# First layer of a five-layer graph network: dense input read from a transposed copy, and a ring of high and low parts scattered by 256-column products

## The chip, the cores and the metric

One core of one Trainium2 chip runs the whole program. The metric is the time of one execution on the device, in microseconds (us). The kernel before took 5494.6 us, the median of three runs (5491.9 to 5495.12).

The engines named here are PE (TensorE, the matrix engine, with PEld for its weight loads), DVE (VectorE), ACT (ScalarE), POOL (GpSimd) and SP (SyncE, which only issues transfers).

## The reference

Five graph layers (SAGE convolutions) run over 100,000 nodes and 50,000 edges that are sorted by destination:

```
def sage(x, Wl, b, Wr):
    mean = segment_sum(x[src], dst) / max(degree, 1)
    return mean @ Wl + b + x @ Wr
x = layernorm(x + sage(relu(sage(x, a1)), a2))
x = layernorm(x + sage(relu(sage(relu(sage(x, b1)), b2)), b3))
```

All values are float32. Layers a1 and a2 are 128 wide, b1 is 128 to 256, b2 is 256 to 256, b3 is 256 to 128. The change is in a1 alone, which has neither a ReLU on its input nor a residual.

## The kernel before

Nodes are cut into 196 groups of 512 (4 tiles of 128). Each layer is one pass over the groups, and the passes run one after the other with a barrier between them. Layers with 128 output columns (a1, a2, b3) are made by `narrow_pass`, those with 256 (b1, b2) by `wide_pass`.

A pass has a dense part and an edge part. Edge tiles of 128 edges are handled two per step. For edge step p, POOL gathers 2 x 128 source rows from HBM by index into `e_rows` (L627), PE transposes them (`turn_edges`, L652), ACT copies the result to `e_full` (L730), PE multiplies by Wl (`project`, L700), and ACT scales by 1/degree and writes the result into a ring of 32 slots in SBUF (`to_ring`, L743). For node group g, SP loads the rows (L580), PE transposes them (`turn_nodes`, L661), ACT copies them (`nodes_full`, L738), and `multiply` (in two halves, u = 0 and 1) adds up in PSUM: 4 dense products with Wr (L686) and 8 scatter products (L690), each a one-hot matrix of 128 x 128 times one slot of the ring. DVE makes the one-hot matrices (`compare`, L792, two of 512 columns for a group) and adds the bias on the way out (`add_up`, L807). SP stores the group (L590).

Edges run 6 steps ahead of nodes (LEAD = 6), so step g works on p = g + 6. What each engine does in a step is written out by hand, and each engine works its own list in order:

- PE: `places(g)` (reads ring slots into registers), `turn_nodes(g+1)`, `multiply(g, 0)`, `project(p-1)`, `turn_edges(p+1)`, `multiply(g, 1)`.
- ACT: `edges_full(p)`, `take_numbers(p+2)` (L725, writes the indices for a gather), `nodes_full(g+1)`, `to_ring(p-1)`.
- POOL: wait for `take_numbers(p+2)`, a marker operation (L623), two gathers for p+2 (L627).
- DVE: `compare(g+1, 0)`, `add_up(g-1)`, `compare(g+1, 1)`.
- SP: load of group g+3, store of group g-1.

`e_rows` has two buffers. `take_numbers(p+2)` comes behind `edges_full(p)` on ACT, and that is what says that a buffer is free. So the gather for p+2 begins in step g and PE takes its rows in step g+1.

Of the kernel before, what the change touches and what calls it, by code (L numbers as in the profile page):

```python
# [12 lines left out]
P = 128  # L13
# [5 lines left out]
LEAD = 6  # L19
BEHIND, AHEAD = 12, 5  # L20
# [494 lines left out]

def narrow_pass(pr, cv):
# [4 lines left out]
    norm = res is not None  # L521
    FUNC = ACT.Relu if cv["relu"] else ACT.Copy
    late = 2 if norm else 1
    with ExitStack() as c:  # L524
        rows_in = pr.sb(c, "m_rows_in", [P, 2, T, kt * P])
        t_full = pr.sb(c, "m_t_full", [P, 2, kt, GROUP])
        onehot = pr.sb(c, "m_onehot", [P, 2, 2 * T, P])
        rows_out = pr.sb(c, "m_rows_out", [P, 2, T, fo])
        e_idx = pr.sb(c, "m_e_idx", [P, 2, 2], I32)
        e_rows = pr.sb(c, "m_e_rows", [P, 2, 2, kt * P])  # L530
        e_full = pr.sb(c, "m_e_full", [P, 2, kt, 2 * P])
        ring = pr.sb(c, "m_ring", [P, RING * fo])
        held = pr.sb(c, "m_held", [1, 1])
        if norm:
# [9 lines left out]
        turned = [pr.ps(c, f"m_turned{i}") for i in range(2)]  # L544
        product = [pr.ps(c, f"m_product{i}") for i in range(2)]
# [3 lines left out]
        rows_here = [pr.counter(f"m_rows_here{i}", 16) for i in range(2)]  # L549
        res_here = [pr.counter(f"m_res_here{i}", 16) for i in range(2)]  # L550
        stored = [pr.counter(f"m_stored{i}", 16) for i in range(2)]
        gathered = [pr.counter(f"m_gathered{i}", 32) for i in range(2)]
        names = ("turned", "full", "onehot", "product", "sum", "stats", "meanvar", "std", "rstd", "shift", "normed",
                 "index", "held", "eturned", "efull", "eproduct", "ring", "eps")
        (s_turned, s_full, s_onehot, s_product, s_sum, s_stats, s_meanvar, s_std, s_rstd, s_shift, s_normed,
         s_index, s_held, s_eturned, s_efull, s_eproduct, s_ring, s_eps) = [pr.counter("m_" + x) for x in names]
        s_done = s_normed if norm else s_sum
        block = c.enter_context(nc.Block())

        def is_last(g):  # L560
            return isinstance(g, int) and g == G - 1

        def has(g, back):

            return g is not None and not (isinstance(g, int) and g < back)

        def turned_before(g, p):

            if p is None:
                return G - 1 if g == G - LEAD else None  # L570
            return None if isinstance(p, int) and p == 0 else p - 1

        def view(t, g, width):
            return t[bass.ds(node_base(pr, g), GROUP), 0:width].rearrange("(t p) f -> p t f", p=P)

        @block.sync
        def _(sp):
            def load_rows(g, s):
                wait(sp, s_turned, (g - 1) * kt)
                sp.dma_start(rows_in[:, s, :, :], view(h, g, kt * P)).then_inc(rows_here[s].sem, 16)  # L580

            def load_res(g, s):
                wait(sp, s_sum, g - 1)
                sp.dma_start(res_in[:, s, :, :], view(res, g, P)).then_inc(res_here[s].sem, 16)

            def store(g, s):
                wait(sp, s_done, g + 1)
                if is_last(g):
                    wait(sp, stored[1 - s], G // 2)
                sp.dma_start(view(out, g, fo), rows_out[:, s, :, :]).then_inc(stored[s].sem, 16)  # L590

            for g in (0, 1):
                load_rows(g, g)
                if norm:
                    load_res(g, g)
            load_rows(2, 0)

            def step(g, s, more):
                if not (isinstance(g, int) and g >= G - 3):
                    load_rows(g + 3, 1 - s)  # L600
                if has(g, late):
                    store(g - late, (s - late) % 2)
                if more and norm:
                    load_res(g + 2, s)

            for g in (0, 1):
                step(g, g, True)
            with sp.Fori(1, G // 2 - 2) as i:
                for s in range(2):
                    step(i * 2 + s, s, True)  # L610
            for g in range(G - 4, G):
                step(g, g % 2, g < G - 2)
            for g in range(G - late, G):
                store(g, g % 2)
# [4 lines left out]
        def _(pool):  # L619
# [5 lines left out]
            def gather(s):  # L625
# [5 lines left out]
            def step(g, p, s, i, j):  # L631
                if p is not None and not (isinstance(p, int) and p + 2 >= G):
                    wait(pool, s_index, p + 3)
                    wait(pool, s_held, p + 1)
                    mark().then_inc(s_held.sem, 1)
                    gather(s)

            mark().then_inc(s_held.sem, 1)
            for p in range(2):
                wait(pool, s_index, p + 1)  # L640
                gather(p)
            steps(pr, pool, step)

        @block.tensor
        def _(pe):
            def turn_edges(p, s, j):
                wait(pe, gathered[s], j + 1)
                wait(pe, s_efull, p)
# [6 lines left out]
            def turn_nodes(g, s, i):  # L655
                wait(pe, rows_here[s], i + 1)
                for k in range(kt):
                    wait(pe, s_full, g * kt + k - 1)
# [6 lines left out]
            def places(g):  # L665

                _, at = nc.values_load_multi_w_load_instructions(
                    pr.t_slot[0:1, bass.ds(g * (2 * T), 2 * T)], engines=[mybir.EngineType.PE], min_val=0,
# [3 lines left out]
            def multiply(g, s, at, u):  # L672
                wait(pe, s_onehot, g * 2 + u + 1)
                bank = product[s]
                if u == 0:
                    ready = g + LEAD - 2
                    wait(pe, s_full, (g + 1) * kt)
                    wait(pe, s_ring, min(ready, G) if isinstance(g, int) else ready)
                    wait(pe, s_sum, g - 1)
                    if norm:  # L680
                        pe.matmul(bank[:, :], pr.two_rows[:, :], cv["bias_row"][:, :, :].rearrange("p a n -> p (a n)"),  # L681
                                  start=True, stop=False, skip_group_check=True)
                for t in range(2 * u, 2 * u + 2):
                    to = bank[:, t * P:(t + 1) * P]
                    for k in range(kt):
                        pe.matmul(to, t_full[:, s, k, t * P:(t + 1) * P], cv["r32"][:, k, :],  # L686
                                  start=(not norm and t == 0 and k == 0), stop=False, skip_group_check=True)
                    for w in range(2):
                        n = 2 * t + w
                        mm = pe.matmul(to, onehot[:, s, n, :], ring[:, bass.ds(at[n] * fo, fo)], start=False,  # L690
                                       stop=(w == 1), skip_group_check=True)
# [3 lines left out]
            def project(p, s):  # L695
                wait(pe, s_efull, p + 1)
                wait(pe, s_ring, p)
# [6 lines left out]
            def step(g, p, s, i, j):  # L704
                if g is None and p == LEAD - 1:
                    turn_nodes(0, 0, 0)
                if g is not None:
                    at = places(g)
                    if not is_last(g):
                        turn_nodes(g + 1, 1 - s, i + s)  # L710
                    multiply(g, s, at, 0)
# [932 lines left out]
```

## Time and profile before

| | |
|---|---|
| median of three runs | 5494.6 us |
| the profiled execution's own time | 5473.94 us |
| span inside it | 5472.3 us |
| PE busy | 5178.4 us (95%) |
| PEld busy | 5110.7 us (93%) |
| DVE busy | 3574.3 us (65%) |
| ACT busy | 2560.0 us (47%) |
| POOL busy | 2278.1 us (42%) |

Busy shares are means over five passes with different limits. A float32 product is two instructions (and two weight loads) in the records, a product of float32r operands one. The duration of a matmul includes its way through the array, so the pace of PE is read from start to start. A bracket behind a row of the timeline is the engine's idle time ahead of it and what ended that.

### The profile page before, as it was taken

How to read it: one execution, taken by the hardware profiler on the slowest of the kernel's cores; microseconds unless marked ns; L12 is line 12 of the kernel's file. 1: busy time of each engine (PE TensorE's matmuls, PEld its weight loads, DVE VectorE, ACT ScalarE, POOL GpSimd, SP SyncE). 2: the span in 40 equal slices, each digit the busy share in tenths (PEclk: the TensorE clock that was granted, in tenths of full speed). 3: DMA queues.
4: the chain of work that ended last, by engine and by line, in shares of the span. 5: the costliest groups of instructions: out<-in, count | busy, mean ns of one | idle time of the engine just before them, and what ended most of it. 6: DMA issues, size and time to landing. Idle time of an engine off the chain costs nothing. (4 is left out here: it accounts for less than half of the span.)

```text
span 5472.3 us, 161658 instructions
## 1 busy us (share of the span) xinstructions
PE 5178.4 (95%) x44358; PEld 5110.7 (93%) x44359; DVE 3574.3 (65%) x9610; ACT 2560.0 (47%) x7254; POOL 2278.1 (42%) x2959
## 2 busy tenths in 40 slices
PE   1999998999999899999989999999999899999999
PEld 0899998889888899999989999999999899999999
DVE  4344444777777788888866666666666455555555
ACT  0343433777777433333333333333333466666666
POOL 1665655555555344444432322322222333333332
PEclk9999999999999999999999999999999999999999
DMA  1555554666667566666655555555555566666666
GB/s 29 150 168 164 172 167 143 202 202 206 205 200 208 164 194 192 194 195 195 193 165 177 173 178 176 174 179 174 174 180 169 178 217 219 217 219 220 216 219 195
DMA packets 1322822, 1006.82 MB, mean 184 GB/s; under 512 B 70406, under 2 KB 1278627, under 8 KB 1322756
## 3 DMA queue, kind: packets, MB, share of 16 engines
q1 hardware_dynamic: 1247044, 825.23, 48.6%
q0 software_dynamic: 75712, 180.76, 10.7%
q8 instruction: 36, 0.59, 0.0%
q14 instruction: 30, 0.25, 0.0%
HBM read 645.58 MB, written 360.13 MB: 184 GB/s over the span
## 5 line engine op out<-in xcount | busy, mean ns | idle before, releaser
L1043 PE MATMUL f_product_b<-f_ring_b,f_onehot_b 128*128 x6272 | 996.5, 281 | 0.0
L690 PE MATMUL m_product_a<-m_ring_a,m_onehot_a 128*128 x6272 | 959.8, 276 | 0.0
L1043 PEld LDWEIGHTS f_product_b<-f_ring_b,f_onehot_b 128*128 128x128 f32 x6272 | 855.8, 188 | 0.0
L1099 ACT ACTIVATE f_ring_b<-f_e_product_b,t_rec_all 128x256 f32 (+1 forms) x784 | 328.9, 471 | 1099.1 <-PE f_e_product_b L1056 1091.1
L792 DVE TENSOR_TENSOR m_onehot_a<-iota_all,t_win_all 128x512 f32<-128x512 f32 x784 | 537.5, 686 | 454.4 <-PE m_product_a L690 388.4
L690 PEld LDWEIGHTS m_product_a<-m_ring_a,m_onehot_a 128*128 128x128 f32 x6272 | 829.5, 193 | 0.0
L1037 PE MATMUL f_product_b<-b_r_all,f_t_hi_b 128*128 128x256 f32 x2352 | 723.2, 307 | 0.0
L1039 PE MATMUL f_product_b<-b_r_all,f_t_lo_b 128*128 128x256 f32 x2352 | 661.0, 281 | 0.0
L1038 PE MATMUL f_product_b<-b_r_all,f_t_hi_b 128*128 128x256 f32 x2352 | 659.4, 280 | 0.0
L686 PE MATMUL m_product_a<-a_r_all,m_t_full_a 128*128 128x128 f32 x3136 | 608.0, 276 | 0.0
L976 POOL TENSOR_TENSOR f_held_b<-ones_all 1x1 f32<-1x1 f32 x390 | 71.4, 183 | 1236.0 <-ACT f_e_idx_b L1081 1157.1
L1158 DVE SCALAR_TENSOR_TENSOR f_ring_b<-f_e_product_b,t_rec_all,f_ring_b 128x256 f32 (+1 forms) x784 | 342.9, 479 | 331.3 <-ACT f_ring_b L1099 321.2
L1094 ACT ACTIVATE f_t_hi_b<-f_turned_b 128x512 fp32r<-128x512 f32 x588 | 330.6, 597 | 446.1 <-PE f_turned_b L1014 442.1
L1152 DVE TENSOR_TENSOR f_rows_out_b<-f_product_b,b_bias_all 128x512 f32<-128x512 f32 x784 | 533.5, 681 | 5.8 <-PE f_product_b L1043 5.8
L1132 DVE SCALAR_TENSOR_TENSOR f_t_lo_b<-f_turned_b,f_t_hi_b 128x512 fp32r<-128x512 f32 x588 | 386.8, 686 | 225.3 <-ACT f_t_hi_b L1094 219.3
L1140 DVE TENSOR_TENSOR f_onehot_b<-iota_all,t_win_all 128x512 fp32r<-128x512 f32 x784 | 502.4, 681 | 0.0
L686 PEld LDWEIGHTS m_product_a<-a_r_all,m_t_full_a 128*128 128x128 f32 x3136 | 491.7, 192 | 8.5
L627 POOL DMA_INDIRECT m_e_rows_a<-in_x_dram,m_e_idx_a x392 | 424.5, 1083 | 140.8 <-issue 135.6
L690 PE MATMUL m_product_b<-m_ring_b,m_onehot_b 128*128 x3136 | 478.2, 275 | 0.0
L686 PE MATMUL m_product_b<-b_r_all,m_t_full_b 128*128 128x128 f32 x3136 | 477.3, 275 | 0.0
L743 ACT ACTIVATE m_ring_a<-m_e_product_a,t_rec_all 128x128 f32 (+1 forms) x784 | 244.8, 363 | 479.1 <-PE m_e_product_a L700 377.1
L980 POOL DMA_INDIRECT f_e_rows_b<-g,f_e_idx_b x392 | 396.3, 1011 | 156.7 <-issue 155.3
(193 smaller groups left out, 12135.2 us busy)
## 6 DMA issues: line engine op xcount, KB each, us to landing
g<-f_rows_out_b SPq DMA_DIRECT2D x392, 512.0 KB
f_rows_in_b<-g SPq DMA_DIRECT2D x196, 512.0 KB
m_rows_in_b<-g SPq DMA_DIRECT2D x196, 512.0 KB
m_rows_in_a<-in_x_dram SPq DMA_DIRECT2D x196, 256.0 KB
h<-m_rows_out_a SPq DMA_DIRECT2D x196, 256.0 KB
m_rows_in_a<-h SPq DMA_DIRECT2D x196, 256.0 KB
m_res_in_a<-in_x_dram SPq DMA_DIRECT2D x196, 256.0 KB
x<-m_rows_out_a SPq DMA_DIRECT2D x196, 256.0 KB
```

What stands on the lines that cost most here:

```text
L627: pool.indirect_dma_start(e_rows[:, s, a, :], None, h, bass.IndirectOffsetOnAxis(ap=e_idx[:, s, a:a + 1], axis=0), bounds_check=bound, oob ...
L686: pe.matmul(to, t_full[:, s, k, t * P:(t + 1) * P], cv["r32"][:, k, :], start=(not norm and t == 0 and k == 0), stop=False, skip_group_che ...
L690: mm = pe.matmul(to, onehot[:, s, n, :], ring[:, bass.ds(at[n] * fo, fo)], start=False, stop=(w == 1), skip_group_check=True)
L792: v.tensor_tensor(onehot[:, s, u * T:(u + 1) * T, :], pr.iota[:, :].unsqueeze(1).to_broadcast([P, T, P]), pr.t_win2[:, bass.ds(g * (2 * T) ...
L980: pool.indirect_dma_start(e_rows[:, s, a, :], None, h, bass.IndirectOffsetOnAxis(ap=e_idx[:, s, a:a + 1], axis=0), bounds_check=bound, oob ...
L1037: pe.matmul(to, t_hi[:, s, k, cols], cv["r2"][:, k, 0, :], start=(k == 0), stop=False)
L1038: pe.matmul(to, t_hi[:, s, k, cols], cv["r2"][:, k, 1, :], start=False, stop=False)
L1039: pe.matmul(to, t_lo[:, s, k, cols], cv["r2"][:, k, 0, :], start=False, stop=False)
L1043: mm = pe.matmul(to, onehot[:, s, n, :], ring[:, bass.ds(at[n] * (2 * fo) + half * fo, fo)], start=False, stop=(w == 1 and half == 1))
L1132: v.scalar_tensor_tensor(out=t_lo[:, s, k, :], in0=turned[(s * kt + k) % 2][:, :], scalar=0.0, in1=t_hi[:, s, k, :].bitcast(F32), op0=ZERO_OP,
L1140: v.tensor_tensor(onehot[:, s, n0:n0 + n, :], pr.iota[:, :].unsqueeze(1).to_broadcast([P, n, P]), pr.t_win2[:, bass.ds(g * (2 * T) + n0, n ...
L1152: v.tensor_tensor(rows_out[:, s, here, :], frm, cv["bias"][:, :].unsqueeze(1).to_broadcast([P, per, fo]), ALU.add).then_inc(s_sum.sem, 1)
```

## The change

In `narrow_pass` for layer a1 alone (`flat=x_flat, split=True`):

1. The host lays out a transposed copy of x, 128 x 100,000. SP loads [128 x 512] of it straight into `t_full` (now three buffers). The PE transposes, the ACT copy of them and `rows_in` are gone. The load of group g waits for the product of group g-3.
2. One-hot and ring are float32r. A ring slot is 256 columns: ACT writes the high part, DVE (`ring_low`) the low part. A scatter product has 256 columns, high and low beside each other, so a group fills two PSUM banks.
3. Two bias products of 256 columns for each group put the bias into PSUM.
4. ACT copies the low halves to SBUF (`low_part`), and DVE adds them to the high halves (`add_up`).
5. The loops of all narrow passes are written with positions in turns of six steps (`At`, `phased`); before, a turn held three pairs of steps, and two steps for SP. The order of the work in a2 and b3 is as before.

The gather's depth `D` is 2 in each pass, as before. The core of the diff:

```diff
+    flat, split = cv.get("flat"), cv.get("split", False)
+    D = cv.get("ahead", 2)
+    R = 3 if flat is not None else 2
+    C = 2 if split else 1
...
+        t_full = pr.sb(c, "m_t_full", [P, R, kt, GROUP])
+        onehot = pr.sb(c, "m_onehot", [P, 2, 2 * T, P], F32R if split else F32)
+        ring = pr.sb(c, "m_ring", [P, RING * C * fo], F32R if split else F32)
+        product = [pr.ps(c, f"m_product{i}", (P, C * 512)) for i in range(2)]
...
+            def load_rows(g):
+                if flat is not None:
+                    wait(sp, s_product, g.n(1 - R))
+                    sp.dma_start(t_full[:, g.slot(R), 0, :], flat[:, bass.ds(base(g), GROUP)]
+                                 ).then_inc(rows_here[g.slot(R)].sem, 16)
...
+            def multiply(g, at, u):
...
+                if split:
+                    pe.matmul(halves(s)[:, 2 * u:2 * u + 2, 0, :], pr.two_rows[:, :], cv["bias_row"][:, 0:2, :],
+                              start=True, stop=False, skip_group_check=True)
                 for t in range(2 * u, 2 * u + 2):
...
+                        pe.matmul(to, t_full[:, r, k, t * P:(t + 1) * P], cv["r32"][:, k, :],
...
+                        mm = pe.matmul(both, onehot[:, s, n, :], ring[:, bass.ds(at[n] * (C * fo), C * fo)],
+                                       start=False, stop=(w == 1), skip_group_check=True)
...
+            def low_part(g):
+                s = g.slot(2)
+                wait(act, s_product, g.n(1))
+                wait(act, s_sum, g.n(-1))
+                act.activation(part[:, s, :, :], halves(s)[:, :, 1, :], ACT.Copy).then_inc(s_part.sem, 1)
...
+            def step(g, p):
+                if split and has(g, 1):
+                    low_part(g.plus(-1))
                 if p is not None:
+                    edges_full(p)
+                    if p.reg is not None or p.off + D < G:
+                        take_numbers(p.plus(D))
+                if flat is None:
+                    if g is None and p.off == LEAD - 1:
+                        nodes_full(At(0))
+                    if g is not None and not is_last(g):
+                        nodes_full(g.plus(1))
                 q = turned_before(g, p)
                 if q is not None:
+                    to_ring(q)
...
+            def ring_low(p):
+                wait(v, s_ringhi, p.n(1))
+                for a in range(2):
+                    at = ((p.n(0, 2) + a) % RING) * (C * fo)
+                    ins = v.scalar_tensor_tensor(out=ring[:, bass.ds(at + fo, fo)],
+                                                 in0=e_product[:, a * fo:(a + 1) * fo],
+                                                 scalar=pr.t_rec[:, bass.ds(p.n(0, 2) + a, 1)],
+                                                 in1=ring[:, bass.ds(at, fo)].bitcast(F32),
+                                                 op0=ALU.mult, op1=ALU.subtract)
+                ins.then_inc(s_ring.sem, 1)
```

## Rows read from the trace of the kernel before

**Rows 1.** Windows: us, PE, PEld, DVE, ACT, POOL busy, PE clock, DMA share, GB/s
```profile
937.00:943.00 6.00, 3.28 (x13) 2.50 (x12) 0.00 (x0) 2.47 (x10) 4.76 (x8) 0.50 0.18 48
165.00:870.00 705.00, 694.11 (x6148) 686.66 (x6147) 341.69 (x543) 287.50 (x904) 433.16 (x542) 1.00 0.58 168
965.00:1800.00 835.00, 777.12 (x6508) 746.36 (x6507) 613.46 (x2605) 599.81 (x1857) 456.36 (x553) 1.00 0.70 204
4284.00:4290.00 6.00, 3.88 (x32) 3.60 (x32) 0.00 (x0) 2.98 (x9) 4.50 (x7) 1.00 0.33 94
```

**Rows 2.** Timeline, one PE step of a1: start us, us, engine, line
```profile
499.90 0.60 PE L661 MATMUL m_turned_a<-ident_all,m_rows_in_a 128*128 128x128 f32 x4
...
503.68 0.60 PE L661 MATMUL m_turned_a<-ident_all,m_rows_in_a 128*128 128x128 f32 x4
```

**Rows 3.** Timeline, 256-column float32r products (PE) and operations (DVE) in b2
```profile
2204.14 0.64 PE L1043 MATMUL f_product_b<-f_ring_b,f_onehot_b 128*128 x4
2204.61 0.28 PE L1037 MATMUL f_product_b<-b_r_all,f_t_hi_b 128*128 128x256 f32 x1
...
2205.47 0.88 DVE L1158 SCALAR_TENSOR_TENSOR f_ring_b<-f_e_product_b,t_rec_all,f_ring_b 128x256 f32 x2
```

**Rows 4.** Timeline, start of a step of a1 on all engines
```profile
861.65 0.38 ACT L730 ACTIVATE m_e_full_a<-m_e_turned_a 128x256 f32<-128x256 f32 x1
...
861.92 0.21 ACT L725 ACTIVATE m_e_idx_a<-t_src_all 128x2 int32 x1
...
862.28 0.60 PE L661 MATMUL m_turned_a<-ident_all,m_rows_in_a 128*128 128x128 f32 x4
862.29 0.18 POOL L623 TENSOR_TENSOR m_held_a<-ones_all 1x1 f32<-1x1 f32 x1 [0.59 <-ACT m_e_idx_a L725]
862.60 0.69 DVE L792 TENSOR_TENSOR m_onehot_a<-iota_all,t_win_all 128x512 f32<-128x512 f32 x1 [1.89 <-PE m_product_a L690]
...
862.91 0.60 ACT L738 ACTIVATE m_t_full_a<-m_turned_a 128x512 f32<-128x512 f32 x1 [0.79 <-PE m_turned_a L661]
...
862.95 1.23 POOL L627 DMA_INDIRECT m_e_rows_a<-in_x_dram,m_e_idx_a  x1 [0.48 <-issue]
```

**Rows 5.** Timeline, from a gather's end to its transposes: prologue, then a1
```profile
152.10 0.99 POOL L627 DMA_INDIRECT m_e_rows_a<-in_x_dram,m_e_idx_a  x1 [0.31 <-issue]
154.68 0.69 PE L652 MATMUL m_e_turned_a<-ident_all,m_e_rows_a 128*128 128x128 f32 x2 [1.12 <-DMA m_e_rows_a<-in_x_dram,m_e_idx_a]
...
170.14 1.00 POOL L627 DMA_INDIRECT m_e_rows_a<-in_x_dram,m_e_idx_a  x1 [0.30 <-issue]
174.71 0.43 PE L652 MATMUL m_e_turned_a<-ident_all,m_e_rows_a 128*128 128x128 f32 x2 [0.61 <-DMA m_e_rows_a<-in_x_dram,m_e_idx_a]
...
349.50 1.00 POOL L627 DMA_INDIRECT m_e_rows_a<-in_x_dram,m_e_idx_a  x1 [1.97 <-ACT m_e_idx_a L725]
350.20 0.38 SPq L580 DMA_DIRECT2D m_rows_in_a<-in_x_dram  x1
352.87 0.43 PE L652 MATMUL m_e_turned_a<-ident_all,m_e_rows_a 128*128 128x128 f32 x2 [1.09 <-DMA m_e_rows_a<-in_x_dram,m_e_idx_a]
```

**Rows 6.** Timeline of a2: one turn of its gather loop
```profile
1397.11 1.00 POOL L627 DMA_INDIRECT m_e_rows_a<-h,m_e_idx_a  x1 [0.30 <-issue]
1397.38 0.60 PE L661 MATMUL m_turned_a<-ident_all,m_rows_in_a 128*128 128x128 f32 x4
1399.13 0.46 POOL L623 TENSOR_TENSOR m_held_a<-ones_all 1x1 f32<-1x1 f32 x1 [1.02 <-ACT m_e_idx_a L725]
1399.79 1.02 POOL L627 DMA_INDIRECT m_e_rows_a<-h,m_e_idx_a  x1 [0.20 <-issue]
1400.69 0.43 PE L652 MATMUL m_e_turned_a<-ident_all,m_e_rows_a 128*128 128x128 f32 x2 [0.69 <-DMA m_e_rows_a<-h,m_e_idx_a]
1401.11 1.00 POOL L627 DMA_INDIRECT m_e_rows_a<-h,m_e_idx_a  x1 [0.30 <-issue]
1402.33 0.63 PE L661 MATMUL m_turned_a<-ident_all,m_rows_in_a 128*128 128x128 f32 x4
```

More of the change, by code:

```diff
@@ L513, in steps, with __init__, n, slot @@
         step(g, None, g % 2, g // 2, None)
+class At:
+    def __init__(self, off, reg=None):
+        self.off, self.reg = off, reg
+    def n(self, more=0, times=1):
+        at = (self.off + more) * times
+        return at if self.reg is None else self.reg * (PHASES * times) + at
+    def slot(self, depth):
+        return self.off % depth
+    def turn(self, depth):
+        at = self.off // depth
+        return at if self.reg is None else self.reg * (PHASES // depth) + at
+    def plus(self, k):
+        return At(self.off + k, self.reg)
+    def below(self, k):
+        return self.reg is None and self.off < k
+def phased(pr, eng, step):
+    G = pr.groups
+    for p in range(LEAD):
+        step(None, At(p))
+    turns = (G - LEAD) // PHASES
+    for g in range(PHASES):
+        step(At(g), At(g + LEAD))
+    with eng.Fori(1, turns) as turn:
+        for m in range(PHASES):
+            step(At(m, turn), At(m + LEAD, turn))
+    for g in range(turns * PHASES, G - LEAD):
+        step(At(g), At(g + LEAD))
+    for g in range(G - LEAD, G):
+        step(At(g), None)
+def uses(G, depth):
+    return [len(range(n, G, depth)) for n in range(depth)]
 def narrow_pass(pr, cv):
@@ L596, in _ @@
[L596 to L600, printed above, removed]
-                if has(g, late):
[L602 to L610, printed above, removed]
@@ new lines, in load_res, with store @@
+            def load_res(g):
+                wait(sp, s_total, g.n(-1))
+                sp.dma_start(res_in[:, g.slot(2), :, :], view(res, g, P)).then_inc(res_here[g.slot(2)].sem, 16)
+            def store(g):
+                wait(sp, s_done, g.n(1))
+                if is_last(g):
+                    wait(sp, stored[1 - g.slot(2)], G // 2)
+                sp.dma_start(view(out, g, fo), rows_out[:, g.slot(2), :, :]).then_inc(stored[g.slot(2)].sem, 16)
+            ahead = R if flat is not None else 3
@@ new lines, in step @@
+            def step(g, p):
+                if g is None:
+                    if p.off < ahead:
+                        load_rows(p)
+                        if norm and p.off < 2:
+                            load_res(p)
+                    return
+                if g.reg is not None or g.off + ahead < G:
+                    load_rows(g.plus(ahead))
+                if has(g, late):
+                    store(g.plus(-late))
+                if norm and (g.reg is not None or g.off + 2 < G):
+                    load_res(g.plus(2))
@@ L675, in multiply @@
                 if u == 0:
[L676 to L681, printed above, removed]
+                    if flat is not None:
+                        wait(pe, rows_here[r], g.turn(R) + 1)
+                    else:
+                        wait(pe, s_full, g.n(1, kt))
@@ L781, in _, with compare @@
-            steps(pr, act, step)
+            for p in range(D):
+                take_numbers(At(p))
+            phased(pr, act, step)
+            if split:
+                low_part(At(G - 1))
             if norm:
-                normalise(G - 2, 0, G // 2 - 1)
-                deviation(G - 1, 1)
-                normalise(G - 1, 1, G // 2 - 1)
+                normalise(At(G - 2))
+                deviation(At(G - 1))
+                normalise(At(G - 1))
         @block.vector
         def _(v):
-            def compare(g, s, u):
-                wait(v, s_product, g - 1)
+            def compare(g, u):
+                s = g.slot(2)
+                wait(v, s_product, g.n(-1))
```

336 lines of the change are left out of this document (185 added, 151 removed).

## The prediction

> **What bounds the kernel now.** I read the shares of the page first (PE 95%), then windows by stage, then one step of a1 on every engine, then each place where PE waited. In a1 PE is busy 694 of 705 us [rows 1]. The window holds 6148 PE instructions; a step of a1 has 34 (4 transposes, 8 dense, 16 scatter, 4 for the edge projection, 2 edge transposes; float32 products count twice), so 180.8 steps took 705 us: **3.90 us a step**. A step without a stall takes 3.78 us, 0.111 us an instruction, its weight load hidden [rows 2]. The reader is to see that nothing else is near: DVE is busy 342 and ACT 288 of the 705 us. One other thing is close though, and it isn't an engine. It is a **loop of latencies**: take_numbers, POOL's two gathers, the landing of the rows, PE's transposes of them. In a1 it mostly fits under two PE steps. In a2 it doesn't: a step there has 35 PE instructions, so 6508 in 835 us make 4.49 us a step [rows 1], while PE waits for gathered rows [rows 6].
>
> **How that loop is sized, checked on a2.** Call T the start of PE's step g. In a2 the marker comes at T + 1.75, the second gather ends at T + 4.73 (1397.38, 1399.13, 1401.11 + 1.00) [rows 6]. Rows land 2.58 us behind a gather's end (1398.11 to 1400.69), and from these transposes to the next step are 1.64 us (to 1402.33) [rows 6]. The gather of step g is consumed in step g+1, so two steps can't be shorter than 4.73 + 2.58 + 1.64 = 8.95 us, 4.48 us a step. Measured 4.49. That agreement is why I trust the same sum for the new a1.
>
> **The change on PE.** Removed from a step: 4 transposes and 16 scatter instructions. Added: 8 scatter products of 256 columns and 2 bias products of 256. Four such products in b2 take 0.47 us, 0.1175 each [rows 3]. One 256-column product is hardly longer than one of the two instructions it replaces (0.111) [rows 2]. New step: 14 x 0.111 + 10 x 0.1175 = 1.55 + 1.18 = **2.73 us** against 3.78. If PE stayed the bound, 190 steps would give back 190 x (3.90 - 2.73) = 222 us.
>
> **The change on the others.** DVE has three operations of 512 columns (0.69 each [rows 4]) and now two of 128 columns; a pair of 256 columns is 0.88 [rows 3], so at most 2.95 us a step, and less because operations overlap. ACT loses the 512-column copy of turned rows and gets `low_part`, 512 columns too, 0.60 [rows 4]: no change in sum. POOL does the same as before: marker to the end of the second gather 2.98 us [rows 6]. The transfers are as many bytes (640 KB a step, DMA share 0.58 before [rows 1]) in longer rows for the load; at 4.1 us a step they need less than before, whatever long rows bring. Registers and waits of the new loops: a stall of PE's sequencer lies inside the wait found below; in a2 and b3 the list is the same, so I take nothing, between -10 and +10 us. None of these is the next bound.
>
> **What is next: ACT's order.** The new ACT step is `low_part(g-1)`, `edges_full(p)`, `take_numbers(p+2)`, `to_ring(p-1)`. `low_part(g-1)` waits for the whole product of g-1, that is, for T. Before, `edges_full(p)` ran at once behind `to_ring`, 0.63 us ahead of T (861.65 against 862.28), and the indices 0.36 ahead of T [rows 4]. **The added wait holds up both**; behind them on ACT is `to_ring`, and POOL's gathers wait for the indices. So the loop now starts behind T:
> T + 0.32 `low_part` starts (DVE's reaction to the same event, 862.28 to 862.60) [rows 4]; + 0.50 until the next operation starts (0.60 less the 0.10 by which ACT's operations overlap: 861.65 + 0.38 against 861.92 is 0.11) [rows 4]; + 0.27 `take_numbers` starts; + 0.37 marker (861.92 to 862.29); + 0.66 first gather (862.29 to 862.95) [rows 4]; + 1.32 second gather (1399.79 to 1401.11) [rows 6]; + 1.00 its end. That is T + 4.44. Then the landing, then 0.31 for the two transposes after a wait (1.64 in a2 less the 12 instructions behind them, 0.111 each [rows 2, 6]) and half a multiply, 1 x 0.1175 + 4 x 0.111 + 4 x 0.1175 = 1.03, to the start of step g+2. **Two steps = 5.78 us + landing.**
>
> The landing is the disputed term. Quiet, in the prologue, it is 1.59 (153.09 to 154.68). With a load issued 0.30 us ahead of the gather's end (350.20 against 350.50) it is 2.37 (to 352.87). With the burst at the start of a1 it is 3.57 (171.14 to 174.71) [rows 5]. In a2, at a DMA share of 0.70 [rows 1], it is 2.58 [rows 6]. In the new order SP's load of g+3 waits for product g, and the store of g-1 is queued behind it on SP, so both go out in one burst at the next T + 0.3 or so (the rows of the load are needed two steps later, so nobody waits for them); with a step of 4.1 us that is T + 4.4, just when the second gather ends. So the quiet value doesn't fit, the two with a load beside them do: I take their middle, 2.47. Two steps are 8.25, one is **4.13 us**.
>
> The Trainium skill ("DMA: Bandwidth & Descriptors", "Anatomy of one DMA — SWDGE (gpsimd) path") says that a DMA from GpSimd has a fixed part of about 2.0 us, most of it the confirmation of the last write, plus bytes by 436 GB/s. Counted from the gather's end and for 64 KB that would be an estimate of 2.15 us, and a step 3.97 us. The rows here lie on both sides of that.
>
> **The sum.** 190 steps x (4.13 - 3.90) = +43 us. The last six groups have no edges: the old work there was 28 instructions (3.11 us), the new is 8 x 0.111 + 10 x 0.1175 = 2.06: -6 us. Prologue: gathers set it before and after, 0. Total **+37 us**. The profiled execution, 5473.9 (span 5472.3), becomes 5511; the median of the runs stands 21 us above that execution, so I forecast 5494.6 + 37 = **5532 us**.
>
> **The rivals.**
> A. *Short landing (the other side).* If rows land as in the prologue, 1.59 us, a step is 3.69 and the sum 190 x (3.69 - 3.90) - 6 = -46 us: 5449. It decides at 3.93 us a step, a landing of 2.08: below it the change is faster. For it: the load has fewer, longer rows, and the share of DMA falls. Against it: load and store now come in one burst.
> B. *A landing of about 2.1 us*, between the quiet row and the row with a load beside it [rows 5], because a gather's own way to SBUF and back costs most of it and the burst only part: step 3.94, sum +8 - 6 = +2 us: 5497, no change. The page of the Trainium skill named above speaks for this one, and so far the rows don't decide.
> C. *PE or DVE stays the bound*, because the loop isn't closed as I read it: 2.73 to 2.95 a step, -186 to -228 us: 5267 to 5309. Against it: ACT works its list in order, and a2 obeys the same sum.
> D. *A long landing*, 3.57 as at the start of a1: step 4.68, +148 - 6 us: 5637. For it: the two transfers in one burst.
> E. *PE's clock falls.* PE would work 2.73 of 4.1 us, 67%. In the prologue of a2 the granted clock is 0.50 (the 1.2 GHz level) with PE busy 55%; at 4284 to 4290 it stays 1.00 with PE busy 65% [rows 1]. At half clock a step would be 5.46 us: 190 x 1.56 - 6 = +290, 5785. The Trainium skill ("TensorE: Matmul & The Clock Gate", "What's actually happening") has an idle PE fall back to 1.2 GHz; the 65% row speaks against it for waits of a microsecond.
>
> **How the numbers follow.** Forecast (landing 2.2 to 2.9): 0.55. A: 0.15. B (2.0 to 2.2): 0.15. C: 0.04. D and what lies between: 0.08. E: 0.03. A measurement of this kernel can tell about 0.2% (11 us) from no change. That is a landing of 1.97 to 2.20, so same is 0.16; faster is A and C, 0.19; slower 0.65. The range goes from a landing of 1.75 (step 3.77, -31 us: 5464) to one of 3.2 (step 4.49, +106 us: 5601); what it leaves out is the end of A, C, E and the end of D, under 0.2.
>
> **What the profile would show.** Right: `low_part` is the first ACT operation behind each product, 0.3 us after it; the marker comes about 1.5 us behind the start of a PE step; PE idles over 1 us ahead of the edge transposes in nearly each step, put down to the gather's DMA; PE is busy about two thirds of a1; DVE and POOL have idle time; scatter products start every 0.12 us; a1's steady steps take 4.1 us, alternating perhaps but with that mean; a2 to b3 are as before. Wrong: if PE in a1 is busy over 90% the loop isn't closed; if the marker is early, ACT's order was misread; if the second gather's end to the transposes is below 2.1 us, A or B holds; if the granted clock is under 1.00 in a1, E; if a2 or b3 move by over 10 us, the loops that I took at nothing did it.

## The result, and the profile after

| | before | after |
|---|---|---|
| median, same chip | 5494.9 us (8 runs) | 5519.7 us (8 runs) |
| ratio | | 1.0046, 95% interval 1.0034 to 1.0058 |
| profiled execution's own time (span) | 5473.9 (5472.3) | 5521.4 (5519.8) |
| PE busy in the span | 5178.4 (95%) | 5058.7 (92%) |

The changed kernel is slower by 25 us, 0.46%. In the last group of experiments the same two kernels stood at 1.0122 (1.0105 to 1.0139): there the kernel before took 5450.6, the changed one 5516.7. Slower both times, by 25 and by 66 us. The two profiled executions don't stand alike among their runs: the one of the changed kernel is one of its eight (5509.0 to 5529.3), the one of the kernel before, 5473.9, lies under the lowest of its eight (5484.2 to 5500.5). So lengths of the kernel before that are read from its trace may be some 20 us short in all of what its runs take.

The experiments ran in three groups of four, each group on one chip, with the kernel before beside it: 5483.7 us in the first (e1 to e4), 5443.3 in the second (e5 to e8), 5450.6 in the third (e9 to e12). It is the kernel before that moves between groups, so ratios are compared within a group; across groups I compare lengths of passes. There is one trace of the kernel before, so which of its passes moves stays open. Those of b2 and b3 agree in all traces within 5 us, that of b1 within 12, and that of a2, in the kernels that share its code with the changed one, within 18 (840.3 in e6, 858.0 in e3).

Where the time went is read from the first to the last gather of each pass (start of the first, start of the last):

| | a1 | a2 | b1 | b2 | b3 |
|---|---|---|---|---|---|
| before | 754.7 | 866.6 | 911.4 | 1421.3 | 1154.2 |
| after | 816.0 | 850.7 | 914.3 | 1422.5 | 1153.5 |

a1 lost 61 us, a2 won 16, the gap between them 3. The windows of the changed kernel (us; busy time and instructions of PE, PEld, DVE, ACT, POOL; granted clock, DMA share, GB/s), a1 and then a2:

```profile
165.00:850.00 685.00, 526.62 (x3901) 485.90 (x3899) 409.99 (x813) 256.03 (x813) 395.91 (x488) 0.95 0.57 155
1000.00:1830.00 830.00, 782.01 (x6561) 753.39 (x6561) 613.24 (x2602) 602.99 (x1868) 473.65 (x568) 0.99 0.70 206
```

A new a1 step has 24 PE instructions: 3901 of them in 685 us make 4.21 us a step; from transposes 12 to 190 the mean is 4.22 (before 3.90 [rows 1]). PE busy fell, and nothing else is full: the answer must be a wait. The sums of waits in a1, 165 to 850 us (waiter <- releaser: us in total, times, longest):

```profile
POOL m_held_a L687 <- ACT m_e_idx_a L813: 190.9, 98, 4.4
ACT m_part_a L842 <- PE m_product_a L777: 158.7, 127, 4.3
PE m_e_turned_a L730 <- DMA m_e_rows_a<-in_x_dram,m_e_idx_a: 126.7, 78, 2.6
PE m_product_a L766 <- issue: 28.6, 85, 0.9
```

Read upwards from PE: it waits for gathered rows (before, 4.4 us in 5 waits, in the same window), the gathers wait for ACT's indices, and ACT waits in `low_part` (L842) for the product. That is the loop of the prediction. One turn of it, from one `low_part` to the second next, from the timeline of the changed kernel (start, duration; gathers are L692, transposes L730, the marker L687):

```profile
499.94 0.60 ACT L842 ACTIVATE m_part_a<-m_product_a 128x512 f32<-128x512 f32 x1
500.42 0.40 ACT L819 ACTIVATE m_e_full_a<-m_e_turned_a 128x256 f32<-128x256 f32 x1
500.68 0.22 ACT L813 ACTIVATE m_e_idx_a<-t_src_all 128x2 int32 x1
500.99 0.71 POOL L687 TENSOR_TENSOR m_held_a<-ones_all 1x1 f32<-1x1 f32 x1 [2.56 <-ACT m_e_idx_a L813]
501.85 1.03 POOL L692 DMA_INDIRECT m_e_rows_a<-in_x_dram,m_e_idx_a  x1 [0.15 <-POOL m_held_a L687]
...
503.18 1.00 POOL L692 DMA_INDIRECT m_e_rows_a<-in_x_dram,m_e_idx_a  x1 [0.30 <-issue]
...
506.52 0.43 PE L730 MATMUL m_e_turned_a<-ident_all,m_e_rows_a 128*128 128x128 f32 x2 [1.62 <-DMA m_e_rows_a<-in_x_dram,m_e_idx_a]
...
508.03 0.60 ACT L842 ACTIVATE m_part_a<-m_product_a 128x512 f32<-128x512 f32 x1 [1.26 <-PE m_product_a L777]
```

1.05 to the marker, 0.86 to the first gather, 1.33 to the second, 1.00 its own time, 2.34 landing, 1.51 back to `low_part`: 8.09 us for two steps. The step between (a `low_part` at 503.17) cuts them into 3.23 and 4.86; steps alternate all through a1, and their mean is what the loop fixes. By the alternation SP's burst came earlier than forecast: the load went out at 503.30 and the store at 503.83, 0.9 and 0.35 us ahead of the second gather's end, and not just at it.

The same terms as means over 170 gathers of a1 (with the standing term of the prediction; "landing" is from the end of the second gather to the transposes, and so includes PE's lateness where PE came later than the rows):

| term, us | forecast | after | after, third group | split alone (e10) | late load (e11) |
|---|---|---|---|---|---|
| `low_part` to marker | 1.14 | 1.10 | 1.16 | 1.09 | 1.08 |
| to first gather | 0.66 | 0.50 | 0.46 | 0.45 | 0.53 |
| first gather and gap | 1.32 | 1.51 | 1.58 | 1.54 | 1.37 |
| second gather | 1.00 | 1.01 | 1.03 | 1.00 | 1.00 |
| landing | 2.47 | 2.68 | 2.74 | 2.09 | 2.67 |
| transposes to `low_part` | 1.66 | 1.61 | 1.55 | 1.51 | 1.53 |
| two steps | 8.25 | 8.43 | 8.54 | 7.69 | 8.19 |

### The profile page after: what moved, and what is told of

Read it like the earlier page. It is cut to its first block and busy times, and to the rows that moved or that the text cites. A ratio compares the mean times of both kernels' runs of the same rounds, so it can differ in the third digit from the quotient of the medians.

```text
span 5519.8 us, 156983 instructions
## 1 busy us (share of the span) xinstructions
PE 5058.7 (92%) x42398; PEld 4954.4 (90%) x42399; DVE 3697.7 (67%) x10002; ACT 2555.8 (46%) x7254; POOL 2294.4 (42%) x2959
## 5 line engine op out<-in xcount | busy, mean ns | idle before, releaser
L777 PE MATMUL m_product_a<-m_ring_a,m_onehot_a 128*128 x4704 | 867.0, 295 | 0.0
L777 PEld LDWEIGHTS m_product_a<-m_ring_a,m_onehot_a 128*128 128x128 f32 x4704 | 666.8, 196 | 0.0
L896 DVE TENSOR_TENSOR m_onehot_a<-iota_all,t_win_all 128x512 fp32r<-128x512 f32 (+1 forms) x784 | 536.8, 686 | 130.6 <-PE m_product_a L777 116.3
L772 PE MATMUL m_product_a<-a_r_all,m_t_full_a 128*128 128x128 f32 x3136 | 619.3, 280 | 0.0
L772 PEld LDWEIGHTS m_product_a<-a_r_all,m_t_full_a 128*128 128x128 f32 x3136 | 509.5, 196 | 8.4
L834 ACT ACTIVATE m_ring_a<-m_e_product_a,t_rec_all 128x128 f32 (+2 forms) x784 | 244.9, 363 | 514.0 <-PE m_e_product_a L788 403.6
L692 POOL DMA_INDIRECT m_e_rows_a<-in_x_dram,m_e_idx_a x392 | 428.8, 1094 | 113.8 <-issue 100.9
```

What stands on the lines that cost most here:

```text
L692: pool.indirect_dma_start(e_rows[:, s, a, :], None, h, bass.IndirectOffsetOnAxis(ap=e_idx[:, s, a:a + 1], axis=0), bounds_check=bound, oob ...
L772: pe.matmul(to, t_full[:, r, k, t * P:(t + 1) * P], cv["r32"][:, k, :], start=(not norm and not split and t == 0 and k == 0), stop=False, ...
L777: mm = pe.matmul(both, onehot[:, s, n, :], ring[:, bass.ds(at[n] * (C * fo), C * fo)], start=False, stop=(w == 1), skip_group_check=True)
L896: v.tensor_tensor(onehot[:, s, u * T:(u + 1) * T, :], pr.iota[:, :].unsqueeze(1).to_broadcast([P, T, P]), pr.t_win2[:, bass.ds(g.n(0, 2 * ...
```

## The experiments

Every ratio is to the kernel before on the same chip. "a1" is the length from first to last gather as above.

### The loops alone (e1)

The changed kernel with `flat=x_flat, split=True` taken from a1, so that only the rewritten loops are left.

> Layer a1 computed as in the kernel before; only the loops are written with positions in turns of six steps. Theory (the gather loop closes at ACT's new wait): no change, 0 us within 11, a1 3.90 us a step. Rival (part of the loss lies in the rewritten loops): slower by 10 to 25 us, a1's steps longer or PE's idle time put down to issue.

Measured: ratio 0.9947 (0.9926 to 0.9968), a1 745.1, a2 850.2. In this group the rewritten loops are **not** nothing: against the trace of the kernel before a1 is 10 us shorter and a2 16, b1 to b3 stay within 2. Two rows of a2 (1000 to 1700 us), of the kernel before and of this one, show one thing that differs:

```profile
ACT m_ring_a L743 <- issue: 59.8, 42, 1.6
```
```profile
ACT m_ring_a L834 <- issue: 16.0, 12, 1.6
```

ACT stood 42 times ahead of `to_ring` waiting for nothing that the profile shows, now 12 times. That these stalls belong to the loops' turns, and that they are what a2 won by, is argued from the two rows, not shown by a run of its own.

### ACT's order (e2) and a third buffer (e3)

```diff
 def step(g, p):
-    if split and has(g, 1):
-        low_part(g.plus(-1))
     if p is not None:
         edges_full(p)
         if p.reg is not None or p.off + D < G:
             take_numbers(p.plus(D))
+    if split and has(g, 1):
+        low_part(g.plus(-1))
```

> The changed kernel, with low_part moved behind take_numbers in ACT's step; the same work, the same transfers. Theory: the gather loop starts again at the edge transposes. It is transposes 0.31, edges_full about 0.3 later, take_numbers 0.27, marker 0.37, 0.66, 1.32, 1.00 and a landing of 2.4: 6.6 us for two steps, so a1 takes 3.3 to 3.4 us a step where the changed kernel takes 4.22: faster than the changed kernel by 150 to 175 us, about 0.973 of the kernel before. Rival (the clock or the sequencer of PE holds the step, not ACT's order): less than 30 us change.

Measured: 0.9887 (0.9866 to 0.9908), a1 719.4, step 3.72. The same work in another order on ACT is 97 us faster in a1 than the changed kernel. PE's waits for gathered rows fell from 126.7 us to 38.3 (25 waits).

```diff
-            dict(name="a1", ..., flat=x_flat, split=True, ...),
+            dict(name="a1", ..., flat=x_flat, split=True, ahead=3, ...),
```

> The changed kernel with three buffers of gathered rows in a1 (gathers run three steps ahead, not two); ACT's order as in the change. Theory: the same chain has three steps, 8.4 / 3 = 2.8 us, under POOL's 2.98 a step, so POOL or PE with its exposed register loads sets 3.0 to 3.3 us a step: faster than the changed kernel by 175 to 230 us, about 0.965 of before; the landing may be long without harm. Rival (transfers are the bound: load, store and gather share the DMA engines): the landing grows with the pace and the step stays above 3.7.

Measured: 0.9837 (0.9815 to 0.9859), a1 684.3, step 3.53, 132 us less in a1. Here `low_part` stays first; only the loop gets a third step. Both edits hit the loop and nothing else, and both pay: that a1 is bound by the loop through ACT's first wait is **shown**. Both fell short of the step that I expected, though. What was next is in PE's waits, 165 to 850 us, of the kernel with three buffers:

```profile
PE m_product_a L766 <- issue: 34.4, 83, 1.0
PE m_e_product_a L788 <- DVE m_ring_a L928: 22.4, 24, 2.7
PE m_e_turned_a L730 <- ACT m_e_full_a L819: 13.8, 17, 1.2
PE m_product_a L766 <- DVE m_ring_a L928: 12.7, 19, 1.0
```

`edges_full` and `to_ring` are behind `low_part` on ACT, and DVE's `ring_low` behind those. A third buffer frees the gathers from that lateness, not the ring. (The first row, where PE waits for nothing shown at the start of a step, stands where it reads the ring slots into registers; I take it for that.)

### The store ahead of the load (e4)

```diff
-                if g.reg is not None or g.off + ahead < G:
-                    load_rows(g.plus(ahead))
                 if has(g, late):
                     store(g.plus(-late))
+                if g.reg is not None or g.off + ahead < G:
+                    load_rows(g.plus(ahead))
```

> The changed kernel with SP's store of g-1 ahead of the load of g+3, so that store and load go out apart and not in one burst. Theory (the burst makes the landing 2.4 instead of 1.6): the landing falls towards 2.0 and a step by 0.2 us, 20 to 40 us faster than the changed kernel. Rival (a load alone beside the gather's end costs as much, or the landing is the gather's own): no change within 11 us.

Measured: 1.0052 (1.0034 to 1.007), a1 793.5, a2 860.5. The edit is in every narrow pass; a1 is 22 us shorter and a2 10 longer, which isn't clear of the 18 us by which a2 differs without an edit. Inconclusive as a remedy; its landings are used below.

### The wait alone (e5)

```diff
 if p is not None:
+    if cv["name"] == "a1" and has(g, 1):
+        wait(act, s_product, g.n())
     edges_full(p)
```

(on the loops alone, e1.)

> The kernel before with the rewritten loops and one thing more: in a1, ACT waits for the product of group g-1 ahead of edges_full. No split ring, no flat input, no low_part. Theory (the wait by itself closes the gather loop): the loop is the one of the prediction without low_part's 0.50 us, 7.48 us and a half multiply that is longer by 0.3 (8 x 0.111 + 4 x 0.111 against 1.03), so about 3.95 us a step with a landing of 2.4, against 3.85 with the rewritten loops alone: a1's gathers take 755 to 775 us from the first to the last, against 745 with the loops alone, PE waits for gathered rows in a good part of the steps, and the whole is 10 to 30 us above the loops alone. Rival (the low parts and the wide products cost the time, the wait is harmless): 745 us, as with the loops alone, and no wait for gathered rows.

Measured, second group: 0.9998 (0.9989 to 1.0008), a1 753.7, a2 846.6. Against e1 (745.1, 850.2) a1 is 9 us longer, with no firm size across groups. (Its ratio is 0.5% above that of e1 because the kernel before was 40 us faster here; the two spans, 5445.4 and 5442.6, are alike. So the 26 us that the loops win are shown for the first group and not for this one.)

```profile
ACT m_e_full_a L819 <- PE m_product_a L777: 159.8, 176, 2.8
```
```profile
PE m_e_turned_a L730 <- DMA m_e_rows_a<-in_x_dram,m_e_idx_a: 2.6, 3, 1.7
```

The added wait is in all 176 steps, and PE waited for rows 3 times. The rival holds as to the rows: with 34 PE instructions, 3.78 us a step [rows 2], the same wait on ACT is covered. It costs where PE's own step has become shorter than the loop.

### The flat input alone (e6), the split ring alone (e7, e10)

```diff
-            dict(name="a1", ..., flat=x_flat, split=True, ...),
+            dict(name="a1", ..., flat=x_flat, ...),
```

> a1 reads the transposed copy, but keeps the float32 ring and the 128-column scatter products. PE has 30 instructions a step, 30 x 0.111 = 3.33 us. Theory (only low_part's wait closes the loop): without it ACT writes the indices early, the loop is marker at the step's start, 2.98 to the second gather's end, landing 2.4, 0.31 and a half multiply 1.33, 7.0 us for two steps: 3.5 a step, PE the bound or nearly, a1's gathers take 650 to 690 us from first to last and the whole is 2% faster than the changed kernel. Rival (the load straight into t_full, in long rows, disturbs the gathers: landing over 3 us): 4 us a step, 750 us and more.

Measured, second group: 0.985 (0.9833 to 0.9866), a1 676.3, step 3.49, PE waiting for rows 4 times. Against the loops alone a1 is 69 us shorter: **the transposed copy by itself is a gain**, four transposes fewer on a PE that is the bound.

```diff
-            dict(name="a1", ..., flat=x_flat, split=True, ...),
+            dict(name="a1", ..., split=True, ...),
```

> a1 has the ring of high and low parts and low_part, but loads rows and transposes them on PE as before. PE has 4 instructions more than in the changed kernel, 2.73 + 0.44 = 3.17 us. Theory: the loop through low_part is what sets the step, 4.2 us as in the changed kernel, and the transposes lie in the wait: a1's gathers take 805 to 835 us from first to last against 816. Rival (the sum of PE's work still counts, a wait being a fixed amount): 816 + 190 x 0.44 = 900 us. Second rival (the flat load is what lengthens landings): under 780 us.

Measured, second group: 0.9972 (0.9961 to 0.9983), a1 750.2, step 3.87. My theory had said 805 to 835; of the expected lengths only that of the second rival, under 780, holds, and its reason (the flat load lengthens landings) is looked at below. So it was run once more beside the changed kernel, on one chip.

> The changed kernel once more, on the same chip as the next three, so that their landings can be compared with its own. Expected as before: ratio 1.0046 to the kernel before, a1's gathers 805 to 825 us from first to last, 4.2 us a step, landing 2.4 in the steps that wait.

> The split ring without the flat input once more, on the same chip as the changed kernel. It differs in a1 by 4 transposes more on PE and by where SP's load goes out: behind the transposes at the start of a step instead of behind the product, together with the store. Theory (the step is (5.78 us + landing) / 2, and the burst of load and store lengthens the landing): landing 1.9 and 3.87 us a step as before, a1 745 to 765 us, 50 to 70 below the changed kernel in the same job. Rival (the chip of the last job was the faster one, and landings are alike): a1 within 15 us of the changed kernel's, landing 2.4 in both.

Measured, third group: the changed kernel 1.0122 (1.0105 to 1.0139), a1 828.8; the split ring alone 0.9985 (0.9975 to 0.9995), a1 747.0, landing 1.92 in the steps that waited, step 3.85. That is (5.78 + 1.92) / 2, but the loop alone doesn't set it: of 170 steps 137 had no wait for rows and took 3.76 us, 33 had one and took 4.23. With 28 instructions and the pause at the start of a step (below) PE's own list is nearly as long as the loop. With four PE transposes **more**, a1 is 82 us shorter. PE's waits in a1, the changed kernel in this group and then the split ring alone:

```profile
PE m_e_turned_a L730 <- DMA m_e_rows_a<-in_x_dram,m_e_idx_a: 130.3, 74, 3.8
```
```profile
PE m_turned_a L740 <- issue: 43.7, 125, 0.8
PE m_e_turned_a L730 <- DMA m_e_rows_a<-in_x_dram,m_e_idx_a: 23.3, 35, 2.3
```

The table of terms says in which one the two differ: the landing, 2.74 against 2.09, 0.65 of the 0.85 us of two steps. Part of that is PE's lateness. Taken from the last semaphore update of the gather ahead of PE's transposes, the rows were there 2.31 us behind the gather's end in the changed kernel's waiting steps (mean of 78; 1.86 in the 32 of the split ring alone), and 1.91 against 1.70 over all 170. The kernels' loads differ in kind (long rows of the copy, or short rows of x) and in moment: in the changed kernel the load waits for the product, in this one for the first four transposes behind it.

### The load at another moment (e11, e12)

```diff
-                    wait(sp, s_product, g.n(1 - R))
+                    if g.reg is not None or (g.off >= R and g.off + LEAD <= G):
+                        wait(sp, s_eturned, g.n(LEAD))
+                    else:
+                        wait(sp, s_product, g.n(1 - R))
```

> The changed kernel with one wait altered: SP's load for group g+3 waits for the edge transposes of step g+1, which come behind product g on PE, instead of product g itself. The same bytes, the same work on every engine; load and the store queued behind it go out when the gathered rows of that step have been taken. Theory (the burst lengthens the landing): landing 1.6 to 2.0, a step (5.78 + 1.8) / 2 = 3.8 us, a1 735 to 770 us, 45 to 80 below the changed kernel. Rival (the kind of the load, long rows or many bytes, lengthens the landing, not its time): a1 within 15 us of the changed kernel's. Second rival (the burst now meets the first gather of the next step, whose time on POOL grows from 1.0 to 1.5 us): half of the gain or less, 780 to 800.

Measured, third group: 1.0062 (1.0045 to 1.0078), a1 789.3, step 4.09: 40 us less than the changed kernel, but **not** by the landing, which was 2.71 in the waiting steps (2.40 in the changed kernel beside it). The load came out at 501.51, the second gather ended at 501.75: I had moved the burst onto the end of the next gather. What did fall were the long first gathers (over 1.2 us: 41% of them in the changed kernel beside it, 5% here) and PE's clock losses (below). So the length falls into the range of the second rival, 780 to 800, for the opposite of its reason. The windows and PE's wait of this kernel (its lines stand 3 higher):

```profile
165.00:850.00 685.00, 529.99 (x4010) 473.50 (x4008) 406.70 (x834) 264.86 (x835) 394.66 (x503) 1.00 0.58 160
PE m_e_turned_a L733 <- DMA m_e_rows_a<-in_x_dram,m_e_idx_a: 96.3, 121, 2.1
```

> The late load of the kernel above and low_part behind take_numbers on ACT, both in the changed kernel. Theory: the two terms of the loop are independent, 5.78 less 0.50 plus a landing of 1.8, two steps 7.1, 3.55 a step, a1 680 to 710 us. Rival (what held the step at 3.5 us with three buffers holds it here at 3.7 too, as with the order alone): 715 to 730.

Measured, third group: 0.99 (0.9883 to 0.9916), a1 698.1, step 3.61. As the theory had it in length, but not by its reason: the landing wasn't 1.8 (2.73 in the 31 steps that waited), and 140 of 170 steps had no wait for rows and took 3.51 us. PE's longest waits here, 165 to 850 us, are others:

```profile
PE m_product_a L769 <- DVE m_rows_out_a L921: 47.2, 98, 2.2
PE m_e_turned_a L733 <- DMA m_e_rows_a<-in_x_dram,m_e_idx_a: 16.7, 33, 1.2
```

DVE's `add_up` (L921), for which PE waits, itself stands 149.3 us in 125 waits for the store of an earlier group, and the store now goes out later. That the late store is what holds this kernel is argued from these waits, not shown by a run.

Since no run moved the load's moment alone, I sorted the steps of the runs by when SP issued the load and the store, counted from the end of the second gather (steps that waited for rows only, median landing):

| kernel | load issued | store issued | steps | landing |
|---|---|---|---|---|
| after | 1.0 before | 0.3 before | 57 | 2.34 |
| after | 0.5 before | 0.3 behind | 13 | 2.63 |
| e11 | 0.5 before | 0.1 behind | 52 | 2.80 |
| e4 | 1.0 before | 0.95 behind | 51 | 2.20 |
| e10 | at the end | 1.1 behind | 25 | 1.86 |

A load issued 0.5 to 1 us ahead of the gather's end goes with a landing 0.3 to 0.9 us longer than one issued at it. Still further ahead isn't shorter: e11 has 62 more waiting steps with the load 1.0 to 1.5 us ahead, and medians of 2.63 to 2.76.

Does the kind of the load, long rows of the copy or short rows of x, have a part? The traces say no, where they hold both kinds at one moment. Taken from the gather's semaphore and over all steps, not only the waiting ones, the medians are:

| load issued, from the gather's end | long rows | short rows |
|---|---|---|
| 0.8 to 1.2 behind | after 1.57, e6 1.57, e2 1.79 | e10 1.62, e7 1.58, e5 1.60 |
| 0.35 to 0.7 behind | after 1.55, e6 1.53, e2 1.45 | e10 1.63, e7 1.56, e5 1.51 |
| 0.7 to 1.0 ahead | after 2.02, e9 2.24, e2 2.21 | e1 2.16, the kernel before 2.40 |

(The last row has 6 and 7 steps of short rows.) So e10's shorter landing comes from when its load goes out.

### Both, and a2 too (e8)

The order of e2 and `ahead=3` in a1 and a2.

> The changed kernel with low_part behind take_numbers and three buffers for gathered rows in a1, and three buffers in a2 too. In a1 the gather of step g is consumed in step g+2, so the loop allows 8.2 / 3 = 2.7 us a step, PE's own 2.73; three buffers alone gave 684 us from first to last, and both together are expected at 640 to 685 (what holds three buffers at 3.5 us a step isn't the gather loop, so most of it stays). In a2 the loop of 8.95 us goes over three steps, 3.0, and PE's 35 instructions bind, 35 x 0.111 = 3.89 us a step instead of 4.41: a2's gathers from first to last 750 to 790 us instead of 851. The whole: 60 to 110 us below the kernel with three buffers in a1 alone, a ratio of 0.964 to 0.973 to the kernel before. Rival for a2 (another wait, or POOL, holds it): over 830 us.

Measured, second group: **0.9592 (0.9576 to 0.9608)**, 5221.0 against 5443.3 us. a1 604.3 (step 3.11), a2 773.0. PE waited for rows in neither; a1 (165 to 740 us) and a2's window:

```profile
PE m_product_a L766 <- issue: 19.4, 69, 0.5
PE m_product_a L766 <- DVE m_rows_out_a L918: 1.3, 2, 0.7
PE m_product_a L766 <- DVE m_ring_a L928: 0.6, 1, 0.6
```
```profile
800.00:1540.00 740.00, 739.81 (x6453) 731.70 (x6452) 606.79 (x2577) 589.41 (x1840) 457.41 (x552) 1.00 0.77 228
```

The ring's waits of e3 are gone too, which is why a1 came out below the 640 to 685 expected: I had taken what was left in e3 as something apart, and it was the same lateness of ACT. What is left is PE itself, busy 549.11 of 575 us:

```profile
165.00:740.00 575.00, 549.11 (x4435) 517.29 (x4435) 460.95 (x925) 296.66 (x923) 477.90 (x555) 1.00 0.77 210
```

A step's 24 instructions take 2.83 us by the medians from start to start, and another 0.27 goes by at its start: 0.38 us from the last product to the first of the next step, where the kernel before has 0.11. In a2 35 instructions a step and a PE without a pause make 740 x 35 / 6453 = 4.01 us, against 4.43 in the changed kernel (830 x 35 / 6561).

## Why the prediction was right, and where not

**The loop** was right, term by term. Forecast 8.25 us for two steps, measured 8.43; e2 and e3 broke it and a1 fell by 97 and 132 us. The landing, the disputed term, was forecast at 2.47 and came at 2.38 in the 89 steps that waited (2.34 in the turn above). By it alone the step would be (5.78 + 2.38) / 2 = 4.08. Of the two terms that were off, the gap from marker to gather was shorter (0.50 for 0.66) and the first gather with the gap behind it longer (1.51 for 1.32). The Trainium skill ("DMA: Bandwidth & Descriptors", "Anatomy of one DMA — SWDGE (gpsimd) path") gave an estimate of 2.15; the trace has 2.38 with the burst ahead of the gather's end, and 1.92 in e10 with the load at it.

**The clock** was the term that was missing. I had rival E as all or nothing. It came in doses: the granted clock of a1 is 0.95, in the third group 0.93. One dose, from the windows and the timeline of the changed kernel:

```profile
517.00:520.00 3.00, 3.00 (x28) 2.84 (x26) 1.91 (x5) 1.43 (x6) 2.04 (x3) 1.00 0.71 197
520.00:523.00 3.00, 1.31 (x12) 1.12 (x11) 1.59 (x3) 0.17 (x2) 2.44 (x4) 1.00 0.77 219
523.00:526.00 3.00, 2.67 (x17) 2.47 (x17) 1.09 (x3) 1.48 (x5) 0.50 (x1) 0.74 0.30 63
526.00:529.00 3.00, 3.00 (x20) 3.00 (x20) 1.75 (x5) 0.62 (x2) 2.24 (x3) 0.69 0.50 156
529.00:532.00 3.00, 2.80 (x24) 2.53 (x22) 2.49 (x6) 1.59 (x5) 1.49 (x3) 1.00 0.67 185
```
```profile
522.57 0.43 PE L730 MATMUL m_e_turned_a<-ident_all,m_e_rows_a 128*128 128x128 f32 x2 [1.69 <-DMA m_e_rows_a<-in_x_dram,m_e_idx_a]
...
526.40 1.05 PE L788 MATMUL m_e_product_a<-a_l_all,m_e_full_a 128*128 128x128 f32 x4
...
529.85 0.61 PE L788 MATMUL m_e_product_a<-a_l_all,m_e_full_a 128*128 128x128 f32 x4
```

PE waited 1.69 us for rows; behind that the granted clock was 0.74 and 0.69 on the mean of two windows, so at the 1.2 GHz level in a part of each, and four edge products took 1.05 us instead of 0.61. Cut into 78 windows of 10 us (170 to 950), 23 have a clock under 0.97. With PE instructions that lie over an edge counted once, these have 53.3 instructions, the other 55 have 58.3: 4.50 and 4.12 us a step. The 4.12 is the loop as forecast; the doses add 0.10 on the mean, some 20 us in a1. (A step that waits long is slow anyway, so by this split they are 20 at most; no run took them away alone.)

**The sum.** Forecast for a1: 190 x (4.13 - 3.90) = +43. Measured +61: loop -9 (4.08), clock up to +20, and 7 or more that no row places. The tail -3 for -6. **The loops' rewriting** was taken at nothing, -10 to +10; a2 is 16 us shorter, outside that (between the two traces; in the second group e5, with the rewritten loops too, is no faster than the kernel before), and in a1 nothing, since there PE was no longer the bound (e1: -10 where it is). b1 to b3 moved by 3 us together. With 2 us that lie between the passes the profiled executions differ by +47, for +37 forecast.

**From the profile to the median** was the other step that failed. I added 21 us because the median of the runs before stood that far over its profiled execution, and carried that over to the kernel after. But the profiled execution of the kernel before was faster than all eight of its runs; that of the changed kernel, 5521.4, is 2 us from the median, 5519.7. So +47 by the profiles is +25 by the medians: errors of opposite sign (a1 +18, for which the clock's doses are the likeliest cause; a2 -16; this step -23) made the forecast of 5532 come within 12 us. The side was right for the stated reason; the closeness is partly luck.

**The rivals.** A (a short landing makes it faster) didn't happen in this kernel. The nearest to it is e10, with a landing of 1.92 and 0.9985, but there most steps are held by PE's own list. B needed 2.0 to 2.2. C fell: the loop is closed. D didn't come: long landings (over 3.2) are rarer than one in ten waiting steps.

**The signs named in advance.** Right: `low_part` first behind the product, PE idle ahead of the edge transposes by over 1 us (126.7 us in 78 waits), alternating steps with a mean of 4.2, and register loads inside the wait (28.6 us at L766, while the loop's terms leave no room for them; with the loop opened, in e3, they stand free: 34.4). Off: the marker came 1.0 to 1.1 us behind PE's start of a step, not 1.5, since PE's first product is itself held up by the registers. PE busy is 77% and not two thirds: the busy time includes the way through the array; by starts it is 2.83 of 4.22 us, 67%. Scatter products were to start every 0.12 us: of a tile's two scatter and two dense instructions the two scatter products start 0.20 us apart and the next dense one 0.12 behind, 0.46 us for the four, so 0.12 is the mean and not the distance. "In nearly each step" was wrong: the waits fall on every second one, 78 in some 163.

## What to carry to other kernels

When an engine that is the bound is made faster, write down the loops of latencies under it before and after: the wait that the new work adds (here ACT's, for a product) is free while the old bound covers it (0 to 9 us in e5) and costs 60 us when it no longer does. Put what has to wait for this step behind what feeds the next one in an engine's list, or give the loop one more buffer; together they took a1 from 816 to 604 us. Parts of a change that are each good or harmless (a1 with the loops alone 745, flat alone 676, split alone 747 to 750) can lose together (816 to 829), so measure them apart.

## What the runs showed of the hardware

- **Waits of PE and its clock.** In the changed kernel 54 of the 78 waits for rows between 165 and 850 us are 1.5 us or longer (57 of 74 in the third group), and the granted clock is 0.95 (0.93). In e11 3 of 121 are, in e10 4 of 35, and the clock is 1.00 in both, though PE is busy for the same 530 us in e11. The Trainium skill ("TensorE: Matmul & The Clock Gate", "What's actually happening") has an idle PE fall back to 1.2 GHz; here the waits of e11, 0.8 us on the mean, didn't do it, and behind the one of 1.69 us shown above it did.
- **A gather's own time.** In the changed kernel the second gather took 1.00 us nearly always, the first 1.03 or up to 1.54: over 1.2 us in 25% of the steps, 41% in the third group. It is the moment of SP's transfers that goes with it: 36 of the 45 long ones are among the 67 steps in which the store went out about 0.75 us ahead of the gather, and none among the 24 in which it went out 1.4 us or more ahead.
- **A landing isn't one number.** Counted from the gather's end it was 1.86 us with the load issued at that end and 2.80 with the load 0.5 us ahead of it, in kernels of one group, for the same 2 x 64 KB (medians of the waiting steps).
- **The reference moves more than the effect.** The kernel before differed by 44 us between the first comparison and the last (5494.9, 5450.6), the changed one by 3 (5519.7, 5516.7). No run shows why.
